# Chunk states, squares and pooling of a convolution-attention-Mamba block moved between engines

## The reference, cut to what matters

```python
h = group_norm(x); q, k, v = split(h @ qkv_w.T + qkv_b)
x = x + softmax(q @ k.T / sqrt(128)) @ v @ proj_w.T + proj_b          # block 1
u = layer_norm(x)                                                     # block 2
z, xBC, dt = split(u @ in_w.T); dt = softplus(dt + dt_bias)
xs, Bm, Cm = split(silu(causal_conv4(xBC)))
def step(state, (dt_t, x_t, B_t, C_t)):                               # 1024 tokens
    state = state * exp(dt_t * A) + (dt_t * x_t) * B_t
    return state, state . C_t
y = scan(step) + Dp * xs
y = y * silu(z)
y = y * rsqrt(mean(y * y, axis=-1) + eps) * rms_w
out_img = y @ out_w.T
pooled = mean(out_img, over tokens)
hdn = relu(pooled @ se1_w.T + se1_b)
attn = sigmoid(hdn @ se2_w.T + se2_b)
return x + out_img * attn
```

## Time and profile before

| | us |
|---|---|
| median of 3 runs | 271.27 (271.21 to 273.44) |
| the profiled execution, whole | 272.0 |
| its span, first to last instruction | 269.8 |
| TensorE busy | 254.5 (94%), weight loads 224.3 (83%) |
| VectorE busy | 223.4 (83%), 516 instructions |
| ScalarE busy | 208.1 (77%), 414 instructions |
| GpSimd busy | 115.8 (43%), 114 instructions |

### The profile page before, as it was taken

The page is one execution under the profiler, slowest core; times in us unless marked ns, Lnnn a source line. Parts: engine busy times, 40 slices in busy tenths (PEclk is TensorE's granted clock), DMA queues, the critical chain, the costliest instruction groups (busy, mean ns, idle before and its releaser), DMA issues. The chain is left out here.

```text
span 269.8 us, 6198 instructions
## 1 busy us (share of the span) xinstructions
PE 254.5 (94%) x1992; PEld 224.3 (83%) x1992; DVE 223.4 (83%) x516; ACT 208.1 (77%) x414; POOL 115.8 (43%) x114
## 2 busy tenths in 40 slices
PE   2999999999999999999999999999999999989791
PEld 2989997998899889988899789888988798777680
DVE  4689746565598498999999999999989999799933
ACT  2347577989999875898887799767988889998361
POOL 8010021206402730235289742572286269758440
PEclk9999999999999999999999999999999999999997
DMA  6930000000040340000133300051005100101103
GB/s 177 395 145 4 0 0 4 2 0 0 11 149 5 108 129 2 0 2 0 38 125 112 126 2 0 6 173 64 0 2 193 45 4 2 39 0 42 39 4 117
DMA packets 10987, 15.29 MB, mean 57 GB/s; under 512 B 1515, under 2 KB 5708, under 8 KB 10956
## 3 DMA queue, kind: packets, MB, share of 16 engines
q1 hardware_dynamic: 10412, 14.69, 16.2%
q10 hardware_dynamic: 544, 0.21, 0.3%
HBM read 12.70 MB, written 2.20 MB: 55 GB/s over the span
## 5 line engine op out<-in xcount | busy, mean ns | idle before, releaser
L1169 PE MATMUL attn_out<-values,pT 128*128 128x129 f32 x512 | 65.6, 275 | 0.1
L1169 PEld LDWEIGHTS attn_out<-values,pT 128*128 128x128 f32 x512 | 62.6, 191 | 3.6 <-issue 1.7
L986 DVE TENSOR_REDUCE neg_max<-scores 128x1 f32<-128x1024 f32 x32 | 39.0, 1219 | 16.1 <-PE scores L1169 16.0
L655 ACT ACTIVATE probs<-scores,neg_max 128x512 f32<-128x512 f32 x64 | 42.4, 684 | 9.1 <-DVE neg_max L986 9.0
L661 ACT ACTIVATE pT<-bank 128x512 f32<-128x512 f32 x64 | 37.6, 594 | 14.0 <-PE bank L1247 13.9
L1247 PE MATMUL bank<-ident,probs 128*128 128x128 f32 x256 | 37.7, 273 | 0.0
L1247 PEld LDWEIGHTS bank<-ident,probs 128*128 128x128 f32 x256 | 30.3, 141 | 4.5 <-issue 1.4
L1169 PE MATMUL scores<-h_hi,q_hi 128*128 128x512 f32 x64 | 31.7, 496 | 0.0
L567 POOL TENSOR_TENSOR ln_rstd<-ln_var,neg_half 128x4 f32<-128x4 f32 x8 | 11.3, 1412 | 45.5 <-DVE ln_var L1008 45.5
L1079 DVE TENSOR_TENSOR_SCAN L<-L,ident 128x512 f32<-128x512 f32 x24 | 30.4, 1274 | 0.0
L581 POOL TENSOR_TENSOR pre<-pre,th 128x512 f32<-128x512 f32 x16 | 22.6, 1410 | 15.1 <-ACT pre L687 8.2
(11 more groups left out here) (219 smaller groups left out, 597.2 us busy)
## 6 DMA issues: line engine op xcount, KB each, us to landing
L<-decay_rows_d SPq DMA_DIRECT2D x24, 256.0 KB, 3.8
res<-in_x_tok SPq DMA_DIRECT2D x4, 512.0 KB, 7.9
out<-res SPq DMA_DIRECT2D x8, 256.0 KB, 2.0
x_all<-in_x SPq DMA_DIRECT2D x3, 512.0 KB, 8.6
decay_in<-decay_rows_d SPq DMA_DIRECT2D x24, 64.0 KB, 3.4
x_all<-in_x SPq DMA_DIRECT2D x2, 256.0 KB, 3.2
winT<-in_in_wT SPq DMA_DIRECT2D x1, 194.0 KB, 7.1
wqkv<-in_qkv_w ACTq DMA_DIRECT2D x1, 192.0 KB, 4.0
```

What stands on the lines that cost most here:

```text
L655: act.activation(probs[:, i % 2, half_of(h)], scores[:, half_of(h)], ACT.Exp, bias=neg_max[:, i:i + 1]).then_inc(exp_done.sem, 1)
L986: V.tensor_reduce(neg_max[:, n:n + 1], scores[:, :], AX.X, ALU.max, negate=True).then_inc(max_ready.sem, 1)
L1169: return T.matmul(o, w, v, start=start, stop=stop)
```

## The change

1. **States by chunk.** st loses its scan. In half 0 it copies the first chunk's state out of PSUM, and for chunks 1 to 3 it runs four `scalar_tensor_tensor` of 32 columns each (one a head): previous state times that head's decay (a per-partition scalar) plus the contribution from PSUM, written into `stateT` itself. Half 1 does three such groups of four, the first of which reads half 0's last state. Each group waits for the semaphore of the one before it. stc is gone, U's identity product is gone, U of half 1 no longer waits for half 0's state, cd writes 16 columns, and the 1024-column memset of `chunk_decay` is gone.
2. **Squares out of transposes.** Ss transposes y2 (4 transposes) with no wait for sq; sq squares each of the four tiles out of PSUM with an accumulator output (4 ScalarE instructions), and ms reads the sums from SBUF.
3. **One pooling product.** os adds all eight tiles in three dependent GpSimd instructions (512, 256, 128 columns), Pl is one product a batch, pl one copy, SeA one product.
4. **First SE layer per token in batch d.** At the start out_w and se1_w are multiplied (wout_tr, wout_ev, wose_mm, wose_ev). For batch d, Hid multiplies y2 with that product (32 columns a tile), hid copies it, and SeA sums it over tokens with y_rstd as the factor, in eight products. os, Pl and pl of batch d are gone.
5. **ORDER** is a new list throughout, with the same steps otherwise, in other places and with other banks.

```diff
 st, VectorE:
-                    V.tensor_tensor_scan(scanned[:, n, :, :].rearrange("s e c -> s (e c)"),
-                                         chunk_decay[:, n, :, :, :].rearrange("s h p c -> s (h p c)"),
-                                         bank[:, :], 0.0, ALU.mult, ALU.add).then_inc(st_ready.sem, 1)
+                    wait(dve, filled["Yo"], b - 1, 2)
+                    if n == 0:
+                        V.tensor_copy(stateT[:, 0, 0, :], bank[:, 0:P]).then_inc(st_step.sem, 1)
+                    for c in range(1, QUAD):
+                        if n == 1 and c == 1:
+                            wait(dve, st_ready, b, 1)
+                            prev = stateT[:, 0, PAD, :]
+                        else:
+                            wait(dve, st_step, b, c if n == 0 else 3 + c - 1)
+                            prev = stateT[:, n, c - 1, :]
+                        for h in range(HEADS):
+                            cols = slice(h * HEADDIM, (h + 1) * HEADDIM)
+                            r = HEADS * (c - n) + h
+                            last = V.scalar_tensor_tensor(stateT[:, n, c, cols], prev[:, cols], chunk_decay[:, n, r:r + 1],
+                                                          bank[:, c * P + h * HEADDIM:c * P + (h + 1) * HEADDIM],
+                                                          ALU.mult, ALU.add)
+                        last.then_inc(st_ready.sem if c == PAD else st_step.sem, 1)
 stc, ScalarE:
-                    act.activation(stateT[:, n, :, :], scanned[:, n, :, :].rearrange("s e c -> s c e"), ACT.Copy
-                                   ).then_inc(stc_ready.sem, 1)
 U, TensorE:
-                    if n == 1:
-                        mm(slots[:, 0, :], ident[:, :], stateT[:, 0, QUAD - 1, :])
 sq, ScalarE:
-                    act.activation(sq[:, :], y2[:, half], ACT.Square).then_inc(sq_ready.sem, 1)
+                    bank = take(act, b, "Ss", n)
+                    for c in range(QUAD):
+                        last = act.activation(sq[:, tile(c)], bank[:, tile(c)], ACT.Square,
+                                              accum_out=sq_sum[:, QUAD * n + c:QUAD * n + c + 1])
 Ss, TensorE:
-                        last = mm(bank[:, tile(c)], sq[:, tile(c)], ones[:, :])
+                        last = T.transpose(bank[:, tile(c)], y2[:, tile(QUAD * n + c)], ident[:, :])
 os, GpSimd:
-                    pool.tensor_tensor(o_sum[:, n, :, :], o_tok[:, QUAD * n:QUAD * n + 2, :],
-                                       o_tok[:, QUAD * n + 2:QUAD * (n + 1), :], ALU.add).then_inc(o_sum_ready.sem, 1)
+                    wait(pool, o_ready, b, 2)
+                    pool.tensor_tensor(o_sum[:, :, :], o_tok[:, 0:QUAD, :], o_tok[:, QUAD:TILES, :], ALU.add).then_inc(os_step.sem, 1)
+                    wait(pool, os_step, b, 1)
+                    pool.tensor_tensor(o_sum[:, 0:2, :], o_sum[:, 0:2, :], o_sum[:, 2:QUAD, :], ALU.add).then_inc(os_step.sem, 1)
+                    wait(pool, os_step, b, 2)
+                    pool.tensor_tensor(o_sum[:, 0, :], o_sum[:, 0, :], o_sum[:, 1, :], ALU.add).then_inc(o_sum_ready.sem, 1)
 Pl, TensorE:
+                    mm(bank[:, 0:1], o_sum[:, 0, :], ones[:, 0:1]).then_inc(done, 1)
 SeA of batch d, TensorE:
+                        if i % QUAD == 0:
+                            wait(pe, y_rstd_ready, b, i // QUAD + 1)
+                            wait(pe, hid_ready, 0, i // QUAD + 1)
+                        last = mm(bank[0:SE, 0:1], hid[:, i, :], y_rstd[:, i:i + 1], i == 0, i == TILES - 1)
```

```diff
-m7d yo1d Y1d@3 g0d Out0d@1 yo_dx1d y1d sq0d o_raw0d g1d Ss0d@0 ms0d sq1d y_pow0d Out1d@1 Ss1d@4 ms1d y_pow1d o0d
-o_raw1d o1d Pl0d@0 fin1c Pl1d@4 pl0d pl1d SeA0d@2 store0c store1c hdn0d SeB0d@1 tha0d gated0d gated1d fin0d fin1d
-store0d store1d
+m6d Hid0d@0 hid0d yo1d Ss0d@3 m7d Y1d@0 sq0d yo_dx1d gated1c y1d g1d Out0d@1 store1b Ss1d@3 store0c Hid1d@2 ms0d sq1d
+y_pow0d o_raw0d ms1d hid1d y_pow1d fin1c o0d store1c Out1d@0 SeA0d@4 hdn0d SeB0d@1 o_raw1d tha0d gated0d fin0d o1d
+store0d gated1d fin1d store1d
```

More of the change, by code:

```diff
@@ L1348, in step @@
                 elif kind == "Yo":
-                    wait(pe, stc_ready, b, n + 1)
+                    wait(pe, st_ready, b, n + 1)
                     wait(pe, bc_ready, b, n + 1)
@@ L1352, in step @@
                     for c in range(1 - n, QUAD):
-                        last = mm(bank[:, tile(c)], stateT[:, n, c - 1 + n, :], BC[:, tile(QUAD * n + c)])
+                        state = stateT[:, 0, c - 1 + QUAD * n, :] if c + QUAD * n <= QUAD else stateT[:, 1, c, :]
+                        last = mm(bank[:, tile(c)], state, BC[:, tile(QUAD * n + c)])
                     last.then_inc(done, 1)
@@ L1376, in step @@
                     last.then_inc(done, 1)
-                elif kind == "Pl":
-                    if b < BATCH - 1:
-                        wait(pe, o_sum_ready, b, n + 1)
-                        tiles = [o_sum[:, n, k, :] for k in range(2)]
-                    else:
-                        wait(pe, o_raw_ready, 0, n + 1)
-                        wait(pe, y_rstd_ready, b, n + 1)
-                        tiles = [o_tok[:, QUAD * n + k, :] for k in range(QUAD)]
-                    bank, done = fill(pe, b, "Pl", n)
-                    for k, t in enumerate(tiles):
-                        factor = ones[:, 0:1] if b < BATCH - 1 else y_rstd[:, QUAD * n + k:QUAD * n + k + 1]
-                        last = mm(bank[:, 0:1], t, factor, k == 0, k == len(tiles) - 1)
+                elif kind == "Hid":
+                    wait_y2(pe, b, n)
+                    pe.wait_ge(wose_step.sem, 2)
+                    bank, done = fill(pe, b, "Hid", n)
+                    for c in range(QUAD):
+                        last = mm(bank[:, c * SE:(c + 1) * SE], y2[:, tile(QUAD * n + c)], wout_se[:, :])
+                    last.then_inc(done, 1)
+                elif kind == "Pl":
+                    wait(pe, o_sum_ready, b, 1)
+                    bank, done = fill(pe, b, "Pl", n)
+                    mm(bank[:, 0:1], o_sum[:, 0, :], ones[:, 0:1]).then_inc(done, 1)
+                elif kind == "SeA" and b == BATCH - 1:
+                    bank, done = fill(pe, b, "SeA", 0)
+                    for i in range(TILES):
+                        if i % QUAD == 0:
+                            wait(pe, y_rstd_ready, b, i // QUAD + 1)
+                            wait(pe, hid_ready, 0, i // QUAD + 1)
+                        last = mm(bank[0:SE, 0:1], hid[:, i, :], y_rstd[:, i:i + 1], i == 0, i == TILES - 1)
                     last.then_inc(done, 1)
                 elif kind == "SeA":
-                    wait(pe, pooled_ready, b, 2)
+                    wait(pe, pooled_ready, b, 1)
                     bank, done = fill(pe, b, "SeA", 0)
-                    mm(bank[0:SE, 0:1], se1T[:, :], pooled[:, 0:1], True, False)
-                    mm(bank[0:SE, 0:1], se1T[:, :], pooled[:, 1:2], False, True).then_inc(done, 1)
+                    mm(bank[0:SE, 0:1], se1T[:, :], pooled[:, 0:1]).then_inc(done, 1)
                 elif kind == "SeB":
```

223 lines of the change are left out of this document (118 added, 105 removed).

## The result

The changed kernel takes 276.19 us (median of four runs) where the kernel before, run beside it, takes 271.24. The ratio is 1.0155, with a 95% interval of 1.009 to 1.022: slower, by 4 us in the ratio's terms and 5 in the medians' (the ratio goes by means, and one run of the kernel before took 273.44). One of the four runs after took 294.13 us, at a granted TensorE clock of 0.85 on average where the others had 0.98 to 0.99; the ratio leaves it out. The forecast was 277.9 in a range of 271.5 to 284.5. The profiled execution took 276.14 us, with a span of 274.0 (before 272.0 and 269.8), so on the profiled scale the change is +4.1 against a forecast of +6.6.

A forecast was written before the change was run, and what follows sets the result against it. VectorE was taken as the bound from 106 to 258 us, TensorE some 10% behind. Second stretch +4.8, third +2.5 and end -0.7 gave +6.6: median 271.27 becomes 277.9 us, range 271.5 to 284.5.

The forecast's parts named there:

- VectorE as the bound from max2c to max7d: From 106 to 216 us VectorE is busy 107.24 of 110 us, so its work sets the time.
- The states: Replacing scans by small VectorE instructions adds 2.4 us a batch, +9.8 in all; +6.2 before 216 us, +3.5 after.
- The third rival: In the new state steps, small instructions cost their whole 0.25 us or GpSimd delays them: 284.5 us, chance 0.10.
- the rule I weighed: Skill page on VectorE: the next operation waits until the pipe is empty, so each small instruction costs its whole 0.25 us.
- The upper bound of +17: State steps on VectorE, if small instructions take their whole 0.25 us with nothing shared: +17 or 18 us.
- The new order "hides nothing" and "doesn't move the load": The new list puts only some 0.7 us more VectorE work ahead of 106 us, so the 26 idle us stay.
- TensorE "some 10% behind": Weight loads at 88% in the first two stretches were read as TensorE having some slack everywhere.
- The rival in which TensorE sets the pace alone: After 106 us TensorE is the bound, so its 5.9 us of relief and 1.0 at the end count: 264.4, chance 0.09.
- The second rival: The new order takes the idle time after 106 us and shortens the first stretch by 4 us: 270.5, chance 0.13.
- Squares: Four ScalarE squares take 1.5 us a half, +7 on ScalarE in all; transposes take 3.6 us off TensorE.
- Pooling and the end: Pooling takes 2.3 us off TensorE, GpSimd's extra is hidden; batch d's end after the last y_rstd gains 1.0 us.
- The memset: Removing the 0.95 us memset at the start gains between 0 and 0.9 us; taken as 0.

The follow-up runs named there:

- states_old: The kernel before, in its old list, with only the states part changed (small VectorE instructions, no ScalarE copies, identity product or memset): 282.88 us, ratio 1.0408.
- strided_old: The kernel before, old list, without ScalarE's state copies; TensorE loads weights from the scan's own layout, every fourth column: 275.89 us, ratio 1.0155.
- tail_old: The kernel before with the chunk-decay memset moved later and the first SE layer per token in batch d, old list with a new end: 271.50 us, ratio 0.9978.
- sq_old3: The kernel before, old list, squares alone changed, with the squaring eight or nine places behind its transposes in batches a to c: 278.62 us, ratio 1.0234.

## Why the prediction was right, and which of its steps were not

The mechanism held: behind max2c VectorE's work sets the time, the states add to it, and the kernel gets slower. But the sum of +6.6 on the profiled scale came out +4.1, and it is nearer to the result than its terms are, which is luck in part. A stretch is as long as VectorE is busy in it and idle in it, so the terms can be set beside the measured ones:

| span, us | forecast | measured |
|---|---|---|
| to max2c (start, then first stretch) | 0 | -1.1 + 1.5 |
| VectorE busy behind max2c | +6.2 + 3.5 | +3.9 + 1.2 |
| VectorE idle behind max2c, end included | -1.4 - 1.0 - 0.7 | -1.1 - 0.3 |
| together | +6.6 | +4.2 |

**VectorE as the bound from max2c to max7d.** Right for the kernel after: 98.5% busy, waits of 0.5 us in the stretch. states_old shows that its work becomes time one for one in the old list.

**The states.** +9.8 forecast, +8.7 measured in busy time, with 2.49 and 2.15 us a step against 2.5 and 2.2. The third rival, small instructions at their whole length, is out: 0.243 long, 0.158 from start to start. The Trainium skill, "VectorE: DVE Perf Modes", section "Two Vector instructions with no wait between them", lets an instruction start before the one in front has finished where it isn't held, and this trace agrees with that section rather than with the rule I weighed. The upper bound of +17 had no ground in the rows of small instructions of the kernel before.

**The new order "hides nothing" and "doesn't move the load".** This is the step that failed most. VectorE's work behind max2c grew by 5.2 us and not by 9.7. The states are 1.0 of the difference. Another 1.8 is other steps' work that is gone (five copies of the pooled column) or now stands ahead of max2c. I had 0.7 for the steps moved there. The last 1.8 is the same steps running shorter, told next. I had also compared the lists only from max0a on and only by VectorE's steps. So I missed TensorE's set-up products and the steps that changed sides of max0a.

**Instructions that run longer beside GpSimd** were left at nothing and went the good way, from 12.5 to 11.3 us; the kinds of instruction that stand equally often in each stretch of both kernels take 1.8 us less behind max2c.

**TensorE "some 10% behind".** Its relief was counted, as 1.4 and 1.0 us of idle time given back for the 5.9 us of work taken off, and the idle time fell by less than that, 1.1 and 0.3 with the end's gain in it. What was wrong is the reading under it. I took 88% for the weight loads as slack, though the earlier trace rows show the same 88% in the first stretch, where the earlier trace rows show VectorE waiting 21.6 us for TensorE. strided_old, paced by TensorE, shows 89.5%. So TensorE in the kernel before had next to no slack: 6.7 us added to it there cost 4.3. In the kernel after its weight loads stand at 83.7% up to max7d, and a us added costs 0.4. The rival in which TensorE sets the pace alone, 264.4, was wrong as well, since VectorE's work counts at 0.8. Neither engine's sum alone gives the time.

**The second rival,** the order as a gain of 7 us, was wrong in its size. But its subject was more important than I took it for. With the old list this code takes 297.55 us. I had compared the lists only by how much work stands ahead of a mark, and that says nothing of who stands behind whom.

**Squares.** 1.5 us a half forecast; four tiles from 264.68 to 265.83 are 1.15. In all the squares take 9.2 us of ScalarE where they took 5.0, so +4.2 and not +7, less the 9.2 of the copies: ScalarE's busy time falls from 208.1 to 202.3 us and isn't level. They are free only with sq in the right place. The path from the last xs to the last y_rstd was to grow by 0.3, and it is 3.43 us against 3.40.

**Pooling and the end.** -1.2 us from y_rstd to th_att (forecast -1.0). tail_old shows that this gain is paid for by the set-up products and by what Hid puts itself ahead of.

**The memset,** taken as 0, stands: no run tells it from 0.

How the new list keeps the engines from waiting for each other was not taken apart further, because no part can be taken out of either list without the list being wrong for it.

## What to carry to other kernels

Don't read a share of 88% as slack before looking at the same column in a stretch where that engine is known to be the bound. Where two engines are both near full, cost relief and load on either at under one for one (0.4 to 0.8 here), and measure the rate by doubling something harmless. Check a sum by its terms, too: length is busy time and idle time of the engine that is the bound, and each can be off while the total is near. In a kernel whose order is written out by hand, an edit and the list are one change: an in-order engine that waits for a result issued just ahead of it costs more (8.8 us for ten places) than the edit takes off TensorE (3.6 us). And when two lists are compared, every engine's steps count, on both sides of each mark.

## What the runs showed that I had not expected

**The accumulator output is an instruction of its own.** Each of the 32 squares is followed by an ACTIVATION_READ_ACCUMULATOR of 0.21 us, 6.7 us in all. They overlap the squares in part, so four tiles take 1.15 us and not 4 x 0.49 (0.28 for a square and 0.21 for the reading).

**The clock falls before the end.** In the kernel before, TensorE is granted the full clock to 266.0 us, and its last product ends at 264.5. In the kernel after it is idle for 2.1 us, waiting for y2 of half 0 of batch d (256.60 to 258.74), and at 260.7 its clock drops to the lower of its two levels (0.50, 1.2 GHz) for 3.4 us in the middle of the last products. TensorE in order of time:

```profile
255.44 1.16 PE L1197 MATMUL bank<-BC,stateT 128*128 128x128 f32 x8
258.74 1.08 PE L1197 MATMUL bank<-wout_se,xs 128*128 128x32 f32 x8 [2.14 <-POOL xs L602]
...
260.44 1.72 PE L1197 MATMUL bank<-L,xdt 128*32 128x128 f32 x32
262.08 2.08 PE L1197 MATMUL bank<-woutT,xs 128*128 128x128 f32 x8
```

and busy time and clock by us (columns as in the first fence):

```profile
257.00:258.00 1.00, 0.00 (x0) 0.00 (x0) 1.00 (x3) 0.00 (x0) 0.58 (x1) 1.00 0.00 0
...
261.00:262.00 1.00, 1.00 (x24) 0.69 (x16) 0.59 (x1) 0.81 (x7) 0.00 (x0) 0.50 0.48 182
262.00:263.00 1.00, 1.00 (x8) 0.92 (x5) 0.69 (x1) 0.00 (x0) 0.00 (x0) 0.50 0.00 0
263.00:264.00 1.00, 1.00 (x7) 1.00 (x7) 0.77 (x2) 0.00 (x0) 0.14 (x1) 0.50 0.00 0
```

Eight passes of the output product take 2.08 us there and 1.14 us three us later, and Y's 32 take 1.72 where they took 1.08 before. Y's 0.6 us lies on the way to the last y. I put the whole at 0.6 to 0.9 us, an estimate; no run takes the wait away to show it. In sq_old3 the clock is at 0.50 from 243 to 246 us, behind 2.6 us in which TensorE has no product (240.0 to 242.6), and again from 267 us, behind stretches in which it is busy for a third of the time or hardly at all (0.35 of the us at 264, 0.04 of that at 266, with a full one between).

**A strided weight load** costs 326 ns and not 191, and the product behind it 393 and not 280.
